# The last slots of an attention kernel: another bank for the output's product, another split of the copies, and products of zeros in other places

## What is computed

```python
scale = 384 ** -0.5
q = (x @ Wq.T).reshape(b, n, 12, 32)
k = (x @ Wk.T).reshape(b, n, 12, 32)
v = (x @ Wv.T + bv).reshape(b, n, 12, 32)
scores = einsum('bqhd,bkhd->bhqk', q, k) * scale + (adj + adj)[:, None]
row_nonzero = any(scores != 0, axis=-1, keepdims=True)
p = nan_to_num(softmax(where(row_nonzero, scores, -inf), axis=-1))
out = einsum('bhqk,bkhd->bqhd', p, v).reshape(b, n, 384)
y = x + out @ Wo.T + bo
result = (y - mean(y)) / sqrt(var(y) + 1e-5)      # over the 384 channels
```

## Time and profile before

| | us |
|---|---|
| median of 3 runs | 640.82 (640.54 to 641.35) |
| the profiled execution | 640.75 |
| its span in the trace | 639.0 |

### The profile page before, as it was taken

How to read it: one execution, slowest core, us unless ns; L and a number is a source line. 1 busy time by engine, 2 the same in 40 slices (tenths; PEclk the granted TensorE clock), 3 DMA queues, 4 the chain that set the end, 5 groups by cost and what they waited for, 6 DMA issues and landing times.

```text
span 639.0 us, 24017 instructions
## 1 busy us (share of the span) xinstructions
PE 621.3 (97%) x8940; PEld 518.5 (81%) x8940; DVE 494.8 (77%) x2319; ACT 518.4 (81%) x1942; POOL 410.5 (64%) x500
## 2 busy tenths in 40 slices
PE   9999999999999999999999999999999999998885
PEld 5788888888888888888888888888888888887663
DVE  4677877887787787787788778778778778877874
ACT  5688888888888888888888898888888888878662
POOL 1575766857666675776666776675767667656551
PEclk9999999999999999999999999999999999998877
DMA  8300313121131311113131021313103111110111
GB/s 307 131 9 11 110 60 109 59 92 47 34 109 61 109 60 62 49 60 109 60 110 57 30 85 59 109 60 109 50 19 104 58 62 59 60 42 21 51 51 51
DMA packets 17973, 46.24 MB, mean 72 GB/s; under 512 B 1984, under 2 KB 7104, under 8 KB 17856
## 3 DMA queue, kind: packets, MB, share of 16 engines
q1 hardware_dynamic: 17424, 44.11, 20.3%
q10 hardware_dynamic: 432, 0.59, 0.3%
HBM read 32.11 MB, written 12.58 MB: 70 GB/s over the span
## 4 chain that ended last, share of the span: by engine, by line
PE 95%; DVE 4%; issue 1%; ACT 0%; POOL 0%; POOLq 0%; DVEq 0%
PE qk_ps L292 33%; PE vo_ps L369 17%; PE vo_ps L324 15%; PE scores_ps L309 9%; PE scores_ps L336 8%; PE att_ps L354 8%; PE scores_ps L342 2%; DVE nscores L505 1%; PE qk_ps L278 1%; PE scores_ps L381 1%; DVE att_t L552 0%; PE vo_ps L381 0%; PE qk_ps L381 0%; DVE v_n L514 0%; DVE stats L564 0%
## 5 line engine op out<-in xcount | busy, mean ns | idle before, releaser
L415 ACT ACTIVATE probs<-nscores,neg_max 128x128 f32<-128x128 f32 x768 | 297.7, 391 | 24.5 <-DVE neg_max L505 24.5
L505 DVE CUSTOM_DVE_ANT_0 nscores<-scores_ps,adj_n 128x128 f32<-128x128 f32 x768 | 166.8, 286 | 3.1 <-PE scores_ps L309 3.1
L415 ACT ACTIVATION_READ_ACCUMULATOR probs<-nscores,neg_max 128x1 f32 x768 | 145.2, 189 | 0.0
L243 POOL TENSOR_TENSOR tree<-nscores 128x768 f32<-128x768 f32 x64 | 120.3, 1880 | 21.2 <-DVE neg_max L505 21.2
L369 PE MATMUL vo_ps<-w_o,att_t 128*128 128x384 f32 x576 | 117.5, 351 | 2.7 <-DVE v_n L514 2.6
L561 DVE TENSOR_TENSOR y<-vo_ps,x_n 128x384 f32<-128x384 f32 x64 | 35.7, 557 | 103.9 <-PE vo_ps L369 103.9
L225 POOL TENSOR_TENSOR x_t<-x_raw,x_t 128x512 fp32r<-128x512 f32 x45 | 59.1, 1314 | 88.1 <-ACT x_t L432 88.1
L369 PEld LDWEIGHTS vo_ps<-w_o,att_t 128*128 128x128 f32 x576 | 106.9, 197 | 9.3 <-DVE att_t L552 3.9
L324 PE MATMUL vo_ps<-w_v,x_t 128*128 128x384 f32 x576 | 111.8, 338 | 0.0
L292 PE MATMUL qk_ps<-x_t,w_q 128*128 128x512 f32 x405 | 110.7, 411 | 0.0
L292 PE MATMUL qk_ps<-x_t,w_k 128*128 128x512 f32 x405 | 110.6, 411 | 0.0
(11 more groups left out here) (55 smaller groups left out, 729.7 us busy)
## 6 DMA issues: line engine op xcount, KB each, us to landing
x_n<-xn SPq DMA_DIRECT2D x32, 384.0 KB, 3.6
out<-out_n SPq DMA_DIRECT2D x32, 384.0 KB, 2.6
x_raw<-xt SPq DMA_DIRECT2D x15, 768.0 KB, 5.6
adj_n<-adj SPq DMA_DIRECT2D x32, 128.0 KB, 2.6
x_raw<-xt SPq DMA_DIRECT2D x3, 256.0 KB, 5.3
nscores<-wq ACTq DMA_DIRECT2D x3, 192.0 KB, 4.0
nscores<-wk SPq DMA_DIRECT2D x3, 192.0 KB, 5.3
probs<-wv SPq DMA_DIRECT2D x1, 576.0 KB, 6.5
```

Source lines behind the costliest of these rows:

```text
L243: nc.gpsimd.tensor_tensor(tree[:, b % 2, :, 0:width], src[:, :, 0:width], src[:, :, width:2 * width], ALU.add).then_inc(tree_step, 1)
L415: last = nc.scalar.activation(probs[:, b % 2, h], nscores[:, b % 2, h], ACT.Exp, bias=neg_max[:, b % 2, h:h + 1], scale=-1.0, accum_out=ro ...
L505: last = nc.vector.tensor_tensor_reduce(out=nscores[:, half, h], in0=scores_ps[j][:, m * P:(m + 1) * P], in1=adj_n[:, b // 2 % 2, half], s ...
```

## The change

From slot 59 on (`ending(b)`: b above 58) these differ:

- The output's product of graphs 58 to 63 goes into `qk_ps[b % 2]` instead of `vo_ps` (`out_bank`). It waits for ACT's last copy out of the key and query banks (58, 59) or for the residual of the graph two before (60 to 63), and no longer for `keep_v`. `values(61)` to `values(63)` wait for the values before them, no longer for the residual.
- In slots 59 to 62 ACT copies three banks of turned rows and DVE one (`low_banks`). In slot 63 it stays at two and two.
- DVE copies its turned bank ahead of `keep_v`.
- In each of slots 59 to 63 one product of zeros runs ahead of `turn(b)`, into the bank that the next output's product is going to use. The two in the old place in slot 63 are gone.
- In slot 63 PE runs `attend(63)` before `project_out(62)`, and DVE does the residual of 62 in slot 64, behind `attention_low(63)`.

And outside of the last slots: three products of zeros instead of four at the start; and the last store is two stores, one for each graph of the last pair.

```diff
--- before.py
+++ after.py
@@ -150,10 +150,27 @@
             if value > 0:
                 eng.wait_ge(semaphore, value)
+        def ending(b):
+            return b > NB - GRP - 2
+        def out_bank(b):
+            return qk_ps[b % 2] if ending(b + 1) else vo_ps
+        def low_banks(b):
+            return 3 if ending(b) and b < NB - 1 else 2
+        def low_copies(b):
+            return sum(low_banks(i) for i in range(b + 1))
+        def high_copies(b):
+            return sum(HPT - low_banks(i) for i in range(b + 1))
         def projected(b):
-            if b < -1 or b > NB - GRP - 2:
+            if b < -1 or ending(b):
                 return (), ()
             tile = (b + 1) // 2 * 3
             if b % 2 == 1:
@@ -207,10 +224,11 @@
                     sp.wait_ge(x_split, KT * (g - 2))
                     sp.dma_start(x_raw[:, g % 2], xt[g]).then_inc(xt_in[g % 2], DMA)
             last = NB // 2 - 1
-            sp.wait_ge(out_ready, NB)
-            sp.dma_start(out[last], out_n[:, last % 2]).then_inc(stored[last % 2], DMA)
             for half in range(2):
-                sp.wait_ge(stored[half], DMA * (NB // 4))
+                sp.wait_ge(out_ready, NB - 1 + half)
+                sp.dma_start(out[last][:, half], out_n[:, last % 2, half]).then_inc(stored[last % 2], DMA)
+            sp.wait_ge(stored[(last - 1) % 2], DMA * (NB // 4))
+            sp.wait_ge(stored[last % 2], DMA * (NB // 4 + 1))
         @block.gpsimd
         def _(pool):
@@ -272,10 +290,10 @@
         @block.tensor
         def _(pe):
-            def run_idle(count):
+            def run_idle(count, bank):
                 for _ in range(count):
-                    nc.tensor.matmul(qk_ps[0][:], zeros[:, 0:P], zeros[:], start=True, stop=True)
+                    nc.tensor.matmul(bank[:], zeros[:, 0:P], zeros[:], start=True, stop=True)
             def project(tile, first, end):
@@ -315,7 +333,7 @@
                 if b == 0:
                     pe.wait_ge(w_split, 1)
                     pe.wait_ge(first_queries, KT)
-                if b < 3:
+                if b < 3 or ending(b - 2):
                     wait(pe, v_ready, b)
                 else:
                     pe.wait_ge(y_ready, b - 2)
@@ -344,8 +362,8 @@
                 last.then_inc(turned, 1)
             def attend(b):
-                pe.wait_ge(turned_low, 2 * (b + 1))
-                pe.wait_ge(turned_high, 2 * (b + 1))
+                pe.wait_ge(turned_low, low_copies(b))
+                pe.wait_ge(turned_high, high_copies(b))
                 pe.wait_ge(v_ready, b + 1)
                 wait(pe, att_split, b)
                 for m in range(KT):
@@ -356,23 +374,28 @@
                                                 start=True, stop=True)
                 last.then_inc(pv_done, 1)
+            def free_out_bank(b):
+                if not ending(b + 1):
+                    pe.wait_ge(v_ready, b + 3)
+                elif not ending(b - 1):
+                    pe.wait_ge(kept, (NG - 1) * TILES)
+                else:
+                    pe.wait_ge(y_ready, b - 1)
             def project_out(b):
                 pe.wait_ge(att_split, b + 1)
                 if b == 0:
                     pe.wait_ge(w_split, 2)
-                if has(b + 2):
-                    pe.wait_ge(v_ready, b + 3)
-                else:
-                    pe.wait_ge(y_ready, b)
+                free_out_bank(b)
                 for k in range(KT):
                     for n, (a, c) in enumerate(TERMS):
-                        last = nc.tensor.matmul(vo_ps[:, 0:HID], att_t[:, a, k], w_o[:, c, k],
+                        last = nc.tensor.matmul(out_bank(b)[:, 0:HID], att_t[:, a, k], w_o[:, c, k],
                                                 start=(k == 0 and n == 0),
                                                 stop=(k == KT - 1 and n == len(TERMS) - 1))
                 last.then_inc(oproj_done, 1)
             pe.wait_ge(zeroed, 1)
-            run_idle(4)
+            run_idle(3, qk_ps[0])
             for k in range(KT):
                 pe.wait_ge(first_split, 3 * k + 3)
                 for t in range(TILES):
@@ -392,16 +415,21 @@
                     project(tile, first, end)
                 if has(b + 1):
                     values(b + 1)
+                if ending(b) and has(b):
+                    free_out_bank(b - 1)
+                    run_idle(1, out_bank(b - 1))
                 if has(b):
                     turn(b)
                 for tile, first, end in behind:
                     project(tile, first, end)
-                if has(b - 1):
+                if b == NB - 1:
+                    attend(b)
                     project_out(b - 1)
-                if has(b):
-                    attend(b)
-                if b == NB - 1:
-                    run_idle(2)
+                else:
+                    if has(b - 1):
+                        project_out(b - 1)
+                    if has(b):
+                        attend(b)
         @block.scalar
         def _(act):
@@ -434,7 +462,7 @@
             def keep_turned_low(b):
                 act.wait_ge(turned, b + 1)
                 wait(act, pv_done, b)
-                for j in range(2):
+                for j in range(low_banks(b)):
                     nc.scalar.activation(turned_rows(j), turned_bank(j), ACT.Copy).then_inc(turned_low, 1)
             def attention_high(b):
@@ -516,7 +544,7 @@
             def keep_turned_high(b):
                 dve.wait_ge(turned, b + 1)
                 wait(dve, pv_done, b)
-                for j in range(2, HPT):
+                for j in range(low_banks(b), HPT):
                     nc.vector.tensor_copy(turned_rows(j), turned_bank(j)).then_inc(turned_high, 1)
             def find_scale(b):
@@ -541,8 +569,8 @@
             def normalise(b):
                 dve.wait_ge(pv_done, b + 1)
-                dve.wait_ge(turned_low, 2 * (b + 1))
-                dve.wait_ge(turned_high, 2 * (b + 1))
+                dve.wait_ge(turned_low, low_copies(b))
+                dve.wait_ge(turned_high, high_copies(b))
                 nc.vector.tensor_tensor(att_ps[:, 0:HID], att_ps[:, 0:HID],
                                         probs_t[:, HEADS:].rearrange("p m q -> p (m q)"),
                                         ALU.mult).then_inc(att_done, 1)
@@ -558,7 +586,7 @@
                 dve.wait_ge(oproj_done, b + 1)
                 dve.wait_ge(xb_ready, b + 1)
                 wait(dve, out_ready, b - 1)
-                nc.vector.tensor_tensor(y[:, half], vo_ps[:, 0:HID], x_n[:, b // 2 % 2, half],
+                nc.vector.tensor_tensor(y[:, half], out_bank(b)[:, 0:HID], x_n[:, b // 2 % 2, half],
                                         ALU.add).then_inc(y_ready, 1)
                 dve.wait_ge(y_ready, b + 1)
                 nc.vector.bn_stats(stats[:], y[:, half]).then_inc(stats_done, 1)
@@ -592,13 +620,20 @@
                     find_scale(b)
                 if has(b - 1):
                     attention_low(b - 1)
-                if has(b + 1):
-                    keep_v(b + 1)
-                if has(b):
-                    keep_turned_high(b)
-                if has(b - 1):
+                if ending(b):
+                    if has(b):
+                        keep_turned_high(b)
+                    if has(b + 1):
+                        keep_v(b + 1)
+                else:
+                    if has(b + 1):
+                        keep_v(b + 1)
+                    if has(b):
+                        keep_turned_high(b)
+                if b == NB:
+                    residual(b - 2)
+                if has(b - 1) and b != NB - 1:
                     residual(b - 1)
 # ---- launch: one core ----
 def kernel(x, adj, L0_gnn_Wq, L0_gnn_Wk, L0_gnn_Wv, L0_gnn_bv, L0_gnn_Wo, L0_gnn_bo):
```

## The result

The changed kernel takes 632.59 us (median of 4 runs, 631.34 to 632.85) against 640.68 us before (4 runs, 638.52 to 641.35), 8.1 us less. The ratio of the runs is 0.9886 with a 95% interval of 0.9863 to 0.9909: 1.1% faster. (The medians alone would give 1.3%; the next paragraph shows how the one of before can shift.) The profiled execution is the fastest of the four, 631.34 us with a span of 629.5.

The account below looks back on a forecast made before the run. PE's work bounds most of the span; late slots are bound by a chain of waits and a half-clock product. Loops 7.5, last outputs 1.2, store 0.4 and start 0.4 sum to 9.5 us: forecast 631.4 us, range 629.6 to 636.8.

Parts of the forecast that it names:

- The bank: Late slots: the output's product starts about 0.04 us behind the low part instead of 0.61, saving 0.57 us a slot.
- The zeros: Late slots: one product of zeros, at most 0.99 us in PE's wait, keeps the full clock for all four output products.
- The forecast 7.82: Late slots' loop from add to add: 6.01 + 0.04 + 1.77 = 7.82 us against 9.75, four loops giving 7.7 us.
- The late residual rows: Late slots: their load, issued behind the later store, may hold POOL; 0.2 us taken off, leaving 7.5 for the loops.
- The copies: Late slots: ACT's third copy adds some 0.46 us, DVE has one less; attend still waits for PE, not ACT.
- ACT's slack: Late slots: ACT ends 1.83 us into the next loop, where the attention's high part wants it at about 1.9.
- The last two outputs: Add of 61 to add of 63, 12.26 us before: gain 1.2 us, between bounds 0.7 and 2.1.
- product of 62 lies beside that: Slot 63: product of 62 (0.8 + 1.66) fits within the 2.68 us from attend to low part's end.
- expected the clock to drop there: Slot 63, between zeros and attend(63): only 60 transposes for some 4 us, so the clock drops; gain then 0.7 us.
- The start: Kernel start: three zeros let PE's first product start 0.87 us earlier, worth half, 0.4 us; bounds 0.87 and -1.2.
- The store: Kernel end: the last store carries half the bytes, gaining 0.4 us, between nothing and 0.49.

Follow-up runs that it names:

- the second profiled execution: The changed kernel timed once more, unchanged, on one chip with its two-buffer variant: median 632.54 us of 6 runs, this profiled execution 632.49 us.
- the profile that lost 1.5 us at 22 us: The changed kernel without the five products of zeros ahead of turn in slots 59 to 63: median 637.09 us of 10 runs, this profiled execution 640.67 us.

## Why the prediction came out right, and where it did not

The median is 1.2 us above the forecast. The sum of the profile, 9.50 us, meets the forecast's 9.5 to the second digit, and that is luck: no term is met so closely, the tail's came out by two errors, and the profiled execution is the fastest of its four, set against one from the third of the four groups of the kernel before.

**The bank**: right. From add to product 6.62 us became 6.06, and the forecast had 0.57 for that. No run has everything but the bank; the number comes from profiles with and without the wait for `keep_v`.

**The zeros**: right, and shown from both sides: taken out they cost 4.5 us in the medians, put in alone they gave 3.9. The loop is 6.03 + 0.04 + 1.87 = 7.94 us. The forecast 7.82 took the product's 1.77 us to its reader from slot 56; 1.87 to 1.89, the value of the last product in the earlier trace rows, was the right one. A likely reason is that nothing stands in PE's queue ahead of it in the late slots; no run tests that. The late residual rows, for which I took 0.2 us off, cost nothing.

How much the transposes weigh stays open. The drop in slot 63 came behind 2.29 of 3.40 us busy, of which half were zeros and the rest mostly transposes, and a wait of 1.37 us; in another execution the same work kept the clock. The Trainium skill (TensorE: Matmul & The Clock Gate, Part 4: PE-mode transpose) says that transposes don't count as busy in the way other products do. The drop fits that, but no run here took the transposes away, so it stays untested.

**The copies**: costed at nothing, and worth nothing. ACT's slack, forecast at 0.07 us, is 0.19.

**The last two outputs**: the forecast of 1.2 met 1.07 by luck. The step that failed is "product of 62 lies beside that": I let the product of 62 run beside ACT's high part of 63, but there is one `att_t`, and the high part waits for the product that reads it. The order of the change puts that product behind `attend`, so the wait became part of the chain: 1.23 us from the row scale's end. I had also expected the clock to drop there, and in the profiled execution it didn't. The two errors cancel in that one. In the second profiled execution, which lies at the median, the clock does drop, both prices are paid, and the stretch takes 12.75 us, 0.5 more than before. That would also explain a median 1.25 us above the profiled run and 1.2 above the forecast of 631.4. The clocks on record bear it out, with six of ten executions at the second profile's clock and time; and of four profiles with this order of PE in slot 63 and the late zeros, one keeps the clock (11.19 us) and three lose it (12.71, 12.75 and 13.67). Where the unprofiled ones lost it is not shown.

**The start**: 0.4 forecast, 0.65 in the profile, nothing to be told in the medians. I had taken half of the head start, since the first product would run at the lower clock; it came 0.69 us earlier and took 0.95 us instead of 1.25, so nearly all of it arrived. With three zeros PE starts within 0.1 us of its last operand; with four it is late where the zeros ran slowly for long (first product at 7.53, 7.12 and 7.00) and on time where they sped up early (6.67). The add of 57 lay at 580.4 to 581.1 us with three in all profiles but one, and at 580.6 to 581.5 with four. The one, 582.71, is the profile that lost 1.5 us at 22 us; whether the pause before the first product had a part in that is not known.

**The store**: 0.4 forecast, 0.53 in the profile, and 0.4 to 0.6 between any profile with one store and any with two.

Of the 9.50 us between the two profiles 7.25 lie in the loops, where bank and zeros work; no run has these two alone. The change's new order on PE costs 0.7 us at the full clock, and the third bank on ACT gains nothing. DVE's turned copy ahead of `keep_v` was not tested by itself. With a second buffer and two more products of zeros in slot 63 the kernel takes 2.3 us less on the same chip. I did not try both better orders together with the second buffer.

## To carry to other kernels

At the end of a pipeline the filling work runs out. Here each late slot then paid twice: once for the wait, and once for a product at half clock behind it (3.2 us instead of 1.85). A product of zeros placed where the engine waits anyway cost nothing while the clock was full, and kept it full in all four loops once `keep_v` no longer stood in the chain; with `keep_v` still there it did so in two of four. So shorten the chain first, then fill what is left of the wait. And before two steps are swapped, list every buffer that the second one frees: a single buffer turned a harmless order into a wait of 1.2 us.

## What was not expected of the hardware

The same program meets the clock's drop in some executions and not in others: 631.06 and 634.3 us for the changed kernel on one chip, with the drop in slot 63 in one profile and not in the other, behind the same work. Without the zeros four slots of one execution went into their product with the same 2.06 to 2.08 of 3.30 us busy and came out at four different lengths, 1.85 to 3.23 us. At the start eight records of zeros took 5.24 us in one execution and 6.66 in another, while the granted clock read 1.00 in both. A margin that holds in one profile is no proof; the narrow spread of the kernel with more zeros, 629.58 to 629.9 us, was a better sign than any one trace, though one of the six later runs of it took 632.65, at a mean clock of 0.994.
